# The sum of squares of a LayerNorm moved from ScalarE to VectorE, in an attention and feed-forward kernel

## Chip, cores and metric

The kernel runs on one Trainium2 chip, on all 8 of its cores. Each core does the same work on its own eighth of the data; the cores don't talk to each other. The metric is device time in microseconds (us) of the slowest core.

## The reference

The input x is 16 sequences of 4096 tokens, 1024 features each, in float32. One layer is computed:

```python
q, k, v = x @ Wq + bq, x @ Wk + bk, x @ Wv + bv      # 16 heads of 64
# local attention: a window of 128 tokens looks at itself and the window before it,
# causal, scale 64**-0.5; the first window of a sequence sees itself alone
a = softmax(mask(q k^T / 8)) v
x = layernorm(x + a @ Wo + bo)                        # no gain, no bias, eps 1e-5
x = layernorm(x + x @ W^T + b + (x @ V_r) @ C^T)      # V_r, C: rank 32
```

layernorm(y) is (y - mean) / sqrt(var + eps) over the 1024 features.

## The kernel before

**Work of a core.** A core has 2 sequences, 64 windows of 128 tokens; tokens lie on the 128 partitions. Weights are loaded once and cast to bf16 (the first 195 us or so, with the first x and its transposes). Then one loop runs over gi = 0 ... 65. Iteration gi does the attention of window gi, the output projection and first LayerNorm of window gi-1, and the feed-forward part and second LayerNorm of window gi-2. In every fourth iteration (gi = 0, 4, ..., 60) the projections q, k, v of four windows at once stand ahead of the attention (lines 640 to 685): 256 matmuls of 512 columns, in groups of 8 that take turns in four PSUM banks, p0, p1, ps2, ps3. This text calls them the projection block.

**Order.** Every instruction is emitted by hand in a fixed order for each engine, and each engine works through its own list in that order. `KB.emit` turns the tokens of producers and readers into waits on semaphores. VectorE, ScalarE and GpSimd also wait on their own last instruction before each new one (`CHAINED`). So an instruction on VectorE never starts before the one ahead of it in VectorE's list is done.

**One iteration**, in the order of the lists:

- TensorE: transposes of the attention output `ao` (line 377) and of the normed `x2b` (408); the projection block where due; scores (709), 8 groups; low-rank part (426); output projection (394), 16 matmuls, which this text calls the sweep; softmax sums (766); attention times v (808); low-rank second part (475) and feed-forward (488), 16 matmuls.
- ScalarE: copies of v after the projection block (678); 8 exponentials (730), each on one of 4 score banks; then the ScalarE part of the first LayerNorm (541, 556, 560, 569, 578) and of the second (541, 556, 560, 578).
- VectorE: copies out of the transposes (383, 414); bias adds of the projection block (656); copy of the low-rank part (432); causal mask (747); reciprocal of the sums (774); residual add of the first LayerNorm with row sums (454, two halves); first LayerNorm (537 to 563); scaling of the attention output into `ao` (825, two halves); residual add of the second (514, two halves); second LayerNorm (537 to 563).
- GpSimd: output DMA (526), prefilling y1 with x plus bias (441) and y2 (499), casts of x (595), copies of the last k and v (629, 634).

**LayerNorm** is `_ln`, called once for y1 and once for y2, so 128 times in all. VectorE adds the two half sums (537). ScalarE squares y (128 x 1024, float32) and sums the squares into a column `C_VAR` (541); the squared values themselves go to `aofm` as bf16 and nobody reads them. VectorE squares the sum (548) and forms the variance (551). ScalarE takes logarithm and exponential for the reciprocal root (556, 560). VectorE forms -mean times that (563). ScalarE writes the normed rows (569 for bf16, 578 for float32). The columns in between are all in one small tile `cols`.

The first residual add waits for the reciprocal in VectorE's list; the next iteration's exponentials stand behind line 578 of the second LayerNorm in ScalarE's list; the fourth and later score groups wait for a bank that an exponential has read.

Of the kernel before, what the change touches and what calls it, by code (L numbers as in the profile page):

```python
# [10 lines left out]
AF = mybir.ActivationFunctionType  # L11
ALU = mybir.AluOpType
# [91 lines left out]
def build_program(n_windows=64):  # L104
# [22 lines left out]
    kb = KB()  # L127
# [35 lines left out]
    aofm = S("aofm", [128, NCH, W], BF16)  # L163
# [30 lines left out]
    R = {name: Res() for name in  # L194
         ["xb0", "xb1", "xb2", "xb3", "xfm", "qfm", "kfm", "kprev", "v",
          "vprev", "ao", "aofm", "r16", "y1", "y2",
          "x2_0", "x2_1", "x2b_0", "x2b_1", "x2fm_0", "x2fm_1", "xr",
          "u0", "u1", "p0", "p1", "stgA", "stgB", "stgC",
          "cols1", "cols2", "ident", "m01", "ones"]}
# [8 lines left out]
    with ctx:  # L208
        t = kb.emit("gp", lambda e: e.memset(ident[:], 0.0), inc="gp")
        t = kb.emit("gp", lambda e: e.affine_select(  # L210
            out=ident[:], in_=ident[:], compare_op=ALU.not_equal, fill=1.0,
            base=0, pattern=[[-1, 128]], channel_multiplier=1),
            waits=[t], inc="gp")
# [3 lines left out]
            out=m01[:], in_=m01[:], compare_op=ALU.is_gt, fill=1.0,  # L217
            base=0, pattern=[[-1, 128]], channel_multiplier=1),
            waits=[t], inc="gp")
# [36 lines left out]
        for oc in range(NCH):  # L256
            buf, res = stg[i % 2]
            tok = kb.emit("sy", lambda e, s=wf_h[oc * 128:(oc + 1) * 128, :], b=buf:
                          e.dma_start(out=b[:], in_=s), waits=res.wr(),
                          inc=f"di{i % 2}", n=16)  # L260
            res.did_wr(tok)
            tok = kb.emit("ve", lambda e, b=buf: e.tensor_copy(out=xb[:, 0, :], in_=b[:]),
                          waits=res.rd() + R["xb0"].wr(), inc="ve")
# [7 lines left out]
                for ci in range(NCH)]  # L271
            tok = kb.group("pe", fns,
                           waits=R["xb0"].rd() + R["ident"].rd() + R["p0"].wr(),
                           inc="pe")
            R["xb0"].did_rd(tok)
            R["p0"].did_wr(tok)
            tok = kb.emit("ac", lambda e, oc=oc, pb=p0bf: e.activation(
                wt[:, :, oc * 128:(oc + 1) * 128],
                pb[0:128, 0:1024].rearrange("p (c f) -> p c f", c=NCH), AF.Copy),
                waits=R["p0"].rd(), inc="ac")  # L280
# [3 lines left out]
        for oc in range(NCH):  # L284
            buf, res = stg[i % 2]
            tok = kb.emit("sy", lambda e, s=cm_h[oc * 128:(oc + 1) * 128, :], b=buf:
                          e.dma_start(out=b[:, 0:32], in_=s), waits=res.wr(),
                          inc=f"di{i % 2}", n=16)
            res.did_wr(tok)
            tok = kb.emit("ve", lambda e, b=buf: e.tensor_copy(  # L290
                out=xb[:, 0, 0:32], in_=b[:, 0:32]),
                waits=res.rd() + R["xb0"].wr(), inc="ve")
# [3 lines left out]
            tok = kb.emit("pe", lambda e, pb=p1bf: e.transpose(  # L296
                pb[0:32, 0:128], xb[:, 0, 0:32], ident[:]),
                waits=R["xb0"].rd() + R["ident"].rd() + R["p1"].wr(), inc="pe")
            R["xb0"].did_rd(tok)
            R["p1"].did_wr(tok)  # L300
            tok = kb.emit("ac", lambda e, oc=oc, pb=p1bf: e.activation(
                ct[:, oc * 128:(oc + 1) * 128], pb[0:32, 0:128], AF.Copy),
                waits=R["p1"].rd(), inc="ac")
# [3 lines left out]
        for src_h, dst in [(bq_h, bqc), (bk_h, bkc), (bv_h, bvc)]:  # L307
            for c in range(NCH):
                tok = kb.emit("sy", lambda e, s=src_h[c * 128:(c + 1) * 128], d=dst, c_=c:
                              e.dma_start(out=d[:, c_:c_ + 1],  # L310
                                          in_=s.rearrange("(p o) -> p o", o=1)),
                              inc="dc", n=16)
                w_toks.append(tok)
        tok = kb.emit("sy", lambda e: e.dma_start(out=bo_row, in_=bo_h.rearrange("(o f) -> o f", o=1)), inc="dc", n=16)
        w_toks.append(tok)
        tok = kb.emit("sy", lambda e: e.dma_start(out=bf_row, in_=bf_h.rearrange("(o f) -> o f", o=1)), inc="dc", n=16)
# [3 lines left out]
                          waits=[("dc", rows_di)], inc="ve")  # L320
        for half in range(2):
# [7 lines left out]
                for ci in range(NCH)]  # L329
            tok = kb.group("pe", fns,  # L330
                           waits=[bvb_tok] + w_toks[24:32] + bres.wr(), inc="pe")
            bres.did_wr(tok)
            tok = kb.emit("ve", lambda e, b=bank, h=half: e.tensor_tensor(
                out=bo_row[0:1, h * 512:(h + 1) * 512], in0=b[0:1, 0:512],
                in1=bo_row[0:1, h * 512:(h + 1) * 512], op=ALU.add),
                waits=bres.rd() + [("dc", rows_di)], inc="ve")
            bres.did_rd(tok)
            kb.emit("ve", lambda e, h=half: e.tensor_copy(
                out=bcomb[:, h * 512:(h + 1) * 512],
                in_=bo_row[0:1, h * 512:(h + 1) * 512]), inc="ve")  # L340
        bffn_tok = kb.emit("ve", lambda e: e.tensor_copy(out=bffn[:], in_=bf_row),
                           waits=[("dc", rows_di)], inc="ve")
        for row_bf, bc in [(bcomb, bcomb_bc), (bffn, bffn_bc)]:
            for half in range(2):
                bank = p0 if half == 0 else p1
                bres = R["p0"] if half == 0 else R["p1"]
                tok = kb.emit("pe", lambda e, b=bank, h=half, rb=row_bf: e.matmul(
                    b[:], ones_r[:], rb[:, h * 512:(h + 1) * 512],
                    start=True, stop=True),
                    waits=[("ve", kb.cnt["ve"])] + bres.wr() + R["ones"].rd(),  # L350
                    inc="pe")
                bres.did_wr(tok)
                tok = kb.emit("ve", lambda e, b=bank, h=half, d=bc: e.tensor_copy(
                    out=d[:, h * 512:(h + 1) * 512], in_=b[:]),
                    waits=bres.rd(), inc="ve")
# [175 lines left out]
        def _ln(yres, ybuf, out_f32, out_bf, also_bf, out_res=None,  # L531
                bf_res=None, f32_res=None):
            if not isinstance(out_f32, bass.AP):
                out_f32 = out_f32[:]
            if out_bf is not None and not isinstance(out_bf, bass.AP):
                out_bf = out_bf[:]
            tok = kb.emit("ve", lambda e: e.tensor_tensor(
                out=cols[:, C_SUM:C_SUM + 1], in0=cols[:, C_SUM0:C_SUM0 + 1],
                in1=cols[:, C_SUM1:C_SUM1 + 1], op=ALU.add),
                waits=R["cols1"].rd(), inc="ve")  # L540
            tok = kb.emit("ac", lambda e: e.activation(  # L541
                aofm[:].rearrange("p c f -> p (c f)"), ybuf[:], AF.Square,
                accum_out=cols[:, C_VAR:C_VAR + 1]),
                waits=yres.rd() + R["aofm"].wr() + R["cols2"].wr(), inc="ac")
            yres.did_rd(tok)
            R["aofm"].did_wr(tok)
            sq_tok = tok
            kb.emit("ve", lambda e: e.tensor_tensor(
                out=cols[:, C_M2:C_M2 + 1], in0=cols[:, C_SUM:C_SUM + 1],
                in1=cols[:, C_SUM:C_SUM + 1], op=ALU.mult), inc="ve")  # L550
            tok = kb.emit("ve", lambda e: e.scalar_tensor_tensor(
                out=cols[:, C_VAR:C_VAR + 1], in0=cols[:, C_M2:C_M2 + 1],
                scalar=-1.0 / D, in1=cols[:, C_VAR:C_VAR + 1],
                op0=ALU.mult, op1=ALU.add),
                waits=[sq_tok], inc="ve")
            tok = kb.emit("ac", lambda e: e.activation(  # L556
                cols[:, C_LNV:C_LNV + 1], cols[:, C_VAR:C_VAR + 1], AF.Ln,
                bias=eps_c[:], scale=1.0 / D),
                waits=[tok] + R["ones"].rd(), inc="ac")
            rstd_tok = kb.emit("ac", lambda e: e.activation(  # L560
                cols[:, C_RSTD:C_RSTD + 1], cols[:, C_LNV:C_LNV + 1], AF.Exp,
                scale=-0.5), inc="ac")
            nmr_tok = kb.emit("ve", lambda e: e.tensor_scalar(
                out=cols[:, C_NMR:C_NMR + 1], in0=cols[:, C_SUM:C_SUM + 1],
                scalar1=cols[:, C_RSTD:C_RSTD + 1], scalar2=-1.0 / D,
                op0=ALU.mult, op1=ALU.mult), waits=[rstd_tok], inc="ve")
            R["cols2"].did_wr(nmr_tok)
            if also_bf:
                tok = kb.emit("ac", lambda e, o=out_bf: e.activation(
                    o, ybuf[:], AF.Identity, bias=cols[:, C_NMR:C_NMR + 1],  # L570
                    scale=cols[:, C_RSTD:C_RSTD + 1]),
                    waits=[nmr_tok] + yres.rd() + bf_res.wr(), inc="ac")
                yres.did_rd(tok)
                bf_res.did_wr(tok)
            w_extra = out_res.wr() if out_res is not None else []
            if f32_res is not None:
                w_extra = w_extra + f32_res.wr()
            tok = kb.emit("ac", lambda e, o=out_f32: e.activation(  # L578
                o, ybuf[:], AF.Identity, bias=cols[:, C_NMR:C_NMR + 1],
                scale=cols[:, C_RSTD:C_RSTD + 1]),  # L580
                waits=[nmr_tok] + yres.rd() + w_extra, inc="ac")
            yres.did_rd(tok)
            if out_res is not None:
                out_res.did_wr(tok)
            if f32_res is not None:
                f32_res.did_wr(tok)
            if also_bf:
                R["cols2"].did_rd(tok)
# [23 lines left out]
        for gi in (range(NW + 2) if PHASE >= 1 else []):  # L612
# [12 lines left out]
            if att and wt_ == 0:  # L625
# [16 lines left out]
                for dst, wmat, bias, dres in [(qfm, wq, bqc, R["qfm"]),  # L642
                                              (kfm, wk, bkc, R["kfm"])]:
                    for co in range(NCH):
# [4 lines left out]
                            for ci in range(NCH)]  # L649
# [9 lines left out]
                                          op0=ALU.add),  # L659
# [251 lines left out]
```

How the kernel before makes its waits and increments, by code:

```python
        def run(engine_obj, eng_name):  # L845
            for fn, ws, inc_sem, inc_n in kb.ops[eng_name]:
                for sname, val in ws:
                    engine_obj.wait_ge(sems[sname], val)
                inst = fn(engine_obj)
                if inc_sem:
                    inst.then_inc(sems[inc_sem], inc_n)
```

## Time and profile before

| | |
|---|---|
| median of 3 runs | 2299.39 us (2298.78 to 2299.47) |
| the profiled execution, its own time | 2299.96 us |
| its span, slowest core (core 1) | 2298.4 us (the eight: 2289.9 to 2298.4) |
| mean granted TensorE clock, every core | 0.869 to 0.870 |
| busy: TensorE matmul | 1729.3 us (75%) |
| busy: ScalarE | 855.5 us (37%) |
| busy: VectorE | 783.8 us (34%) |
| busy: GpSimd | 419.8 us (18%) |

Busy is the time in which an engine had an instruction running, as a share of the span. No engine is full. The granted clock is the share of 2.4 GHz that TensorE was given: in any moment it is 1 (2.4 GHz) or 0.5 (1.2 GHz). The span starts with the first instruction and ends with the last; the run's own time has 1.6 us around it.

### The profile page before, as it was taken

The page shows a single profiled execution, that of the slowest core. Times are in us where ns is not written, and L with a number is a line of the kernel's source. Part 1 is how long each engine was busy: PE and PEld are TensorE (multiplying, and loading weights), DVE is VectorE, ACT ScalarE, POOL GpSimd, SP SyncE. Part 2 cuts the span into 40 slices and gives each one's busy share as a digit, 9 for nine tenths or more (in the row PEclk, how much of TensorE's full clock was granted, in tenths as well). Part 3 has the DMA queues.
Part 4 walks back from the last instruction along what each step waited for, and adds up shares of the span by engine and source line. Part 5 has one row for each costly group of instructions (what it writes and reads, how often), then busy time and mean ns, then how long its engine had stood idle before and what let it go on. Part 6 is the DMA issues. An engine that isn't in the chain of part 4 may idle for free.

```text
span 2298.4 us, 37165 instructions; the slowest of 8 cores (2289.9 to 2298.4 us)
## 1 busy us (share of the span) xinstructions
PE 1729.3 (75%) x12924; PEld 884.8 (38%) x12924; DVE 783.8 (34%) x1774; ACT 855.5 (37%) x1381; POOL 419.8 (18%) x297
## 2 busy tenths in 40 slices
PE   0026787887969787787969787887969787887965
PEld 0012444444434444444434343444434444444432
DVE  1112243424333342424343343423333343424332
ACT  2110425335252434434252434435252434434253
POOL 0010022211131221212131221212131221212121
PEclk9987798888979798898989798888979898888977
DMA  5521010201111110201111110201111110201000
GB/s 184 161 70 48 19 56 23 70 12 37 46 47 47 32 62 16 70 18 38 47 47 47 33 61 17 76 11 37 46 47 46 32 61 17 77 10 38 10 29 28
DMA packets 111292, 107.58 MB, mean 47 GB/s; under 512 B 89602, under 2 KB 89602, under 8 KB 111108
## 3 DMA queue, kind: packets, MB, share of 16 engines
q1 hardware_dynamic: 101892, 71.66, 10.9%
q0 software_dynamic: 9216, 33.56, 3.7%
q8 instruction: 105, 1.72, 0.3%
q14 instruction: 79, 0.65, 0.1%
HBM read 54.81 MB, written 33.55 MB: 38 GB/s over the span
## 4 chain that ended last, share of the span: by engine, by line
PE 51%; ACT 20%; DVE 13%; issue 7%; DMA 5%; SPq 2%; DVEq 1%; ACTq 1%; POOL 0%; POOLq 0%
PE p L394 15%; PE p L646 10%; PE ps L646 10%; ACT ep L730 8%; ACT aofm L541 6%; PE ps L668 5%; PE p L668 5%; DVE ao L825 4%; DVE y L454 3%; DVE y L514 3%; PE ps L426 3%; ACT outb L578 3%; PE u L766 2%; SPq L602 2%; ACT cols L556 1%
## 5 line engine op out<-in xcount | busy, mean ns | idle before, releaser
L709 PE MATMUL ps<-qfm,kfm 64*128 64x128 bf16 x1792 | 180.5, 254 | 250.7 <-ACT ep L730 247.3
L394 PE MATMUL p<-wo,aofm 128*128 128x512 bf16 x1024 | 343.0, 510 | 0.0
L541 ACT ACTIVATE aofm<-y 128x1024 bf16<-128x1024 f32 x128 | 135.3, 1057 | 522.7 <-DVE y L454 347.8
L730 ACT ACTIVATE ep<-ps 128x512 bf16<-128x512 f32 x496 | 296.2, 597 | 83.5 <-PE ps L709 8.4
L526 POOL DMA_DIRECT2D out<-outb x64 | 36.7, 573 | 1584.6 <-DVE x2fm L414 1460.4
L488 PE MATMUL p<-wt,x2fm 128*128 128x512 bf16 x1024 | 233.9, 382 | 0.0
L678 ACT CAST v_sb<-p 128x512 bf16<-128x512 f32 x64 | 37.5, 586 | 523.7 <-PE p L668 523.7
L709 PEld LDWEIGHTS ps<-qfm,kfm 64*128 64x128 bf16 x1792 | 110.2, 107 | 299.5 <-issue 294.7
L394 PEld LDWEIGHTS p<-wo,aofm 128*128 128x128 bf16 x1024 | 122.4, 125 | 201.7 <-issue 159.8
L432 DVE CAST xr<-ps 32x128 bf16<-32x128 f32 x64 | 17.8, 279 | 498.9 <-PE ps L426 498.9
L441 POOL TENSOR_TENSOR y<-x_sb,bcomb_bc 128x1024 f32<-128x1024 f32 x64 | 136.5, 2133 | 63.9 <-ACT x L578 59.8
L646 PE MATMUL p<-xfm,wq 128*128 128x512 bf16 x512 | 118.3, 385 | 36.4 <-DMA xfm<-xb 36.4
L488 PEld LDWEIGHTS p<-wt,x2fm 128*128 128x128 bf16 x1024 | 95.3, 98 | 123.1 <-issue 18.4
L499 POOL TENSOR_TENSOR y<-x,bffn_bc 128x1024 f32<-128x1024 f32 x64 | 135.8, 2122 | 12.9 <-POOL y L441 12.7
L668 PE MATMUL ps<-wv,xfm 128*128 128x512 bf16 x512 | 115.7, 379 | 0.0
L646 PE MATMUL ps<-xfm,wq 128*128 128x512 bf16 x512 | 115.7, 379 | 0.0
L646 PE MATMUL p<-xfm,wk 128*128 128x512 bf16 x512 | 115.7, 379 | 0.0
L646 PE MATMUL ps<-xfm,wk 128*128 128x512 bf16 x512 | 115.7, 379 | 0.0
L668 PE MATMUL p<-wv,xfm 128*128 128x512 bf16 x512 | 115.7, 379 | 0.0
L595 POOL CAST xb<-x_sb 128x1024 bf16<-128x1024 f32 x64 | 78.1, 1220 | 201.1 <-DMA x_sb<-x 191.2
L747 DVE TENSOR_TENSOR ep<-ep,m 128x2048 bf16<-128x2048 bf16 x64 | 87.8, 1373 | 74.7 <-ACT ep L730 56.5
L514 DVE SCALAR_TENSOR_TENSOR y<-p,y 128x512 f32<-128x512 f32 x128 | 88.5, 691 | 31.5 <-DVE ao L825 13.9
(89 smaller groups left out, 2012.8 us busy)
## 6 DMA issues: line engine op xcount, KB each, us to landing
x_sb<-x SPq DMA_DIRECT2D x16, 2048.0 KB, 8.3
out<-outb POOLq DMA_DIRECT2D x64, 512.0 KB, 3.1
xfm<-xb SPq DMA_TRANSPOSE x512, 2.3
y<-Wq SPq DMA_DIRECT2D x8, 512.0 KB, 4.3
y<-Wk SPq DMA_DIRECT2D x8, 512.0 KB, 4.0
y<-Wv SPq DMA_DIRECT2D x8, 512.0 KB, 4.5
y<-Wo SPq DMA_DIRECT2D x8, 512.0 KB, 4.6
y<-Wf SPq DMA_DIRECT2D x8, 512.0 KB, 4.3
```

The costliest lines, as they stand in the source:

```text
L394: fns = [(lambda e, ci=ci, b=bank, h=half: e.matmul(b[:], aofm[:, ci, :], wo[:, ci, h * 512:(h + 1) * 512], start=(ci == 0), stop=(ci == N ...
L441: tok = kb.emit("gp", lambda e, w_=wt_, p_=par: e.tensor_tensor(out=y1[:], in0=x_sb[:, p_, w_, :], in1=bcomb_bc[:], op=ALU.add), waits=R[" ...
L488: fns = [(lambda e, ci=ci, b=bank, h=half, pw=pw: e.matmul(b[:], x2fm[:, pw, ci, :], wt[:, ci, h * 512:(h + 1) * 512], start=False, stop=( ...
L499: tok = kb.emit("gp", lambda e, pw=pw: e.tensor_tensor(out=y2[:], in0=x2[:, pw, :], in1=bffn_bc[:], op=ALU.add), waits=R["y2"].wr() + R[f" ...
L514: e.scalar_tensor_tensor(out=y2[:, h * 512:(h + 1) * 512], in0=b[:], scalar=1.0, in1=y2[:, h * 512:(h + 1) * 512], op0=ALU.mult, op1=ALU.a ...
L541: tok = kb.emit("ac", lambda e: e.activation(aofm[:].rearrange("p c f -> p (c f)"), ybuf[:], AF.Square, accum_out=cols[:, C_VAR:C_VAR + 1] ...
L646: fns = [(lambda e, ci=ci, b=bank, co=co, wm=wmat: e.matmul(b[:], wm[:, ci, co * 128:(co + 1) * 128], xfm[:, ci, :], start=(ci == 0), stop ...
L668: fns = [(lambda e, ci=ci, b=bank, tc=tc, h=half: e.matmul(b[:], xfm[:, ci, tc * W:(tc + 1) * W], wv[:, ci, h * 512:(h + 1) * 512], start= ...
L709: e.matmul(b[:, r:r + 128], ks, qs, start=True, stop=True))
L730: tok = kb.emit("ac", lambda e, b=bank, g=g: e.activation(ep[:, g, :], b[:], AF.Exp, scale=0.125), waits=bres.rd() + eres.wr(), inc="ac")
L747: tok = kb.emit("ve", lambda e, epc=ep_cur: e.tensor_tensor(out=epc, in0=epc, in1=m01[:].unsqueeze(1).broadcast_to([128, 16, 128]), op=ALU ...
L825: tok = kb.emit("ve", lambda e, b=bank, bi=bank_i: e.tensor_tensor(out=ao[:, bi * 512:(bi + 1) * 512].rearrange("p (h f) -> p h f", h=8), ...
```

## The change

In `_ln` the squares and their sum are made by VectorE, in one `scalar_tensor_tensor` instruction that computes (y * 1.0) * y and sums it, in place of ScalarE's `activation` with `AF.Square`. Output tile, accumulated column, waits and readers are the same; the token is VectorE's. In VectorE's list the instruction stands behind line 537 and ahead of line 548.

```diff
@@ _ln
                 in1=cols[:, C_SUM1:C_SUM1 + 1], op=ALU.add),
                 waits=R["cols1"].rd(), inc="ve")
-            tok = kb.emit("ac", lambda e: e.activation(
-                aofm[:].rearrange("p c f -> p (c f)"), ybuf[:], AF.Square,
+            tok = kb.emit("ve", lambda e: e.scalar_tensor_tensor(
+                out=aofm[:].rearrange("p c f -> p (c f)"), in0=ybuf[:],
+                scalar=1.0, in1=ybuf[:], op0=ALU.mult, op1=ALU.mult,
                 accum_out=cols[:, C_VAR:C_VAR + 1]),
-                waits=yres.rd() + R["aofm"].wr() + R["cols2"].wr(), inc="ac")
+                waits=yres.rd() + R["aofm"].wr() + R["cols2"].wr(), inc="ve")
             yres.did_rd(tok)
             R["aofm"].did_wr(tok)
             sq_tok = tok
```

## Rows read from the trace of the kernel before

**Rows 1.** The page's chain that ended last: by engine, then by line.

```profile
PE 51%; ACT 20%; DVE 13%; issue 7%; DMA 5%; SPq 2%; DVEq 1%; ACTq 1%; POOL 0%; POOLq 0%
PE p L394 15%; PE p L646 10%; PE ps L646 10%; ACT ep L730 8%; ACT aofm L541 6%; PE ps L668 5%; PE p L668 5%; DVE ao L825 4%; DVE y L454 3%; DVE y L514 3%; PE ps L426 3%; ACT outb L578 3%; PE u L766 2%; SPq L602 2%; ACT cols L556 1%
```

**Rows 2.** Groups of instructions: count | busy us, mean ns | idle before, releaser.

```profile
L394 PE MATMUL p<-wo,aofm 128*128 128x512 bf16 x1024 | 343.0, 510 | 0.0
L541 ACT ACTIVATE aofm<-y 128x1024 bf16<-128x1024 f32 x128 | 135.3, 1057 | 522.7 <-DVE y L454 347.8 <-PE p L475 100.6 <-DVE y L514 66.2
L454 DVE SCALAR_TENSOR_TENSOR y<-p,y 128x512 f32<-128x512 f32 x128 | 88.5, 691 | 21.4 <-DVE r L774 8.3 <-PE p L394 4.9
L747 DVE TENSOR_TENSOR ep<-ep,m 128x2048 bf16<-128x2048 bf16 x64 | 87.8, 1373 | 74.7 <-ACT ep L730 56.5 <-ACT ep L724 18.2
...
L240 DVE CAST wk<-y 128x1024 bf16<-128x1024 f32 x4 | 2.8, 694 | 18.9 <-DMA y<-Wk 18.9
```

**Rows 3.** VectorE's timeline, iteration 26; last, projection block of gi 28: start, us.

```profile
1062.29 0.69 DVE L454 SCALAR_TENSOR_TENSOR y<-p,y 128x512 f32<-128x512 f32 x1
...
1063.09 0.16 DVE L537 TENSOR_TENSOR cols<-cols 128x1 f32<-128x1 f32 x1
1063.36 0.16 DVE L548 TENSOR_TENSOR cols<-cols 128x1 f32<-128x1 f32 x1
1064.39 0.16 DVE L551 SCALAR_TENSOR_TENSOR cols<-cols 128x1 f32<-128x1 f32 x1 [0.87 <-ACT aofm L541]
...
1068.39 0.69 DVE L514 SCALAR_TENSOR_TENSOR y<-p,y 128x512 f32<-128x512 f32 x1 [0.17 <-DVE y L514]
...
1069.20 0.16 DVE L537 TENSOR_TENSOR cols<-cols 128x1 f32<-128x1 f32 x1
...
1070.44 0.16 DVE L551 SCALAR_TENSOR_TENSOR cols<-cols 128x1 f32<-128x1 f32 x1 [0.82 <-ACT aofm L541]
...
1096.47 0.75 DVE L656 TENSOR_SCALAR qfm<-p,bqc 128x512 bf16<-128x512 f32 x1 [0.18 <-DVE x2fm L414]
```

**Rows 4.** Timeline of ScalarE in iteration 26 and into 27.

```profile
1063.14 1.06 ACT L541 ACTIVATE aofm<-y 128x1024 bf16<-128x1024 f32 x1 [6.27 <-DVE y L454]
1064.10 0.19 ACT L541 ACTIVATION_READ_ACCUMULATOR aofm<-y 128x1 f32 x1
...
1069.19 1.06 ACT L541 ACTIVATE aofm<-y 128x1024 bf16<-128x1024 f32 x1 [0.91 <-DVE y L514]
...
1073.14 5.81 ACT L730 ACTIVATE ep<-ps 128x512 bf16<-128x512 f32 x8
```

**Rows 5.** The chain: start, us; sweeps of iterations 4, 21-23, 57-60; projection block gi 28.

```profile
359.52 4.36 PE p L394 x16
...
902.59 5.87 PE p L394 x16
926.50 5.86 PE p L394 x16
950.06 4.34 PE p L394 x16
...
1098.40 3.45 PE p L646 x16
...
2066.21 4.35 PE p L394 x16
2088.24 5.26 PE p L394 x16
2111.55 5.55 PE p L394 x16
2172.45 5.82 PE p L394 x16
```

**Rows 6.** Two of those sweeps as stretches: busy us of each engine, PEclk, DMA.

```profile
926.50:932.36 5.86, 5.86 (x24) 2.24 (x24) 1.50 (x2) 0.94 (x2) 0.73 (x1) 0.60 0.11 24
950.06:954.40 4.34, 4.34 (x24) 1.85 (x24) 1.51 (x2) 0.93 (x2) 0.73 (x1) 0.82 0.01 4
```

## The prediction

> **What bounds the kernel now.** I read the shares of the engines first: none is full. The chain of work that ended last therefore came next. It has TensorE at 51%, ScalarE at 20%, VectorE at 13% and 7% of issue, spread over a dozen lines; the ScalarE square (line 541) alone holds 6% of the span [rows 1]. A chain that keeps changing engines means latency: each step waits for the one before it. The question is whether the square is on that chain in all iterations, and what the replacement takes.
>
> The groups say what the square waits for. ScalarE sat idle 522.7 us ahead of its 128 squares, and the releasers are VectorE's residual adds (454, 514) [rows 2]; the 14 put down to line 475 are the same wait, since 475 itself waits for line 454. ScalarE never holds its square back in the loop. In the timeline of iteration 26 ScalarE had been idle 6.27 us before the first square and 0.91 us before the second [rows 4]. VectorE in turn stood idle 0.87 and 0.82 us for it, with line 551 starting 0.10 us after the sum was read out (1064.10 + 0.19, then 1064.39) [rows 3, 4]. So ScalarE has room, and relieving it of 135 us buys nothing by itself. What counts is when line 551 can start.
>
> From line 551 on all is serial. First LayerNorm: 551, 556, 560, 563, then 825 (which stands behind 563 in VectorE's list), then 514. Second: 551 to 563, then ScalarE's 578, then the exponentials that stand behind it (1073.14 in iteration 26 [rows 4]), of which the fifth frees the bank for line 426, behind which the sweep stands. The sweep ends in line 766, the reciprocal and the next 454. A delay of either line 551 goes into the iteration whole.
>
> One place has cover. In the 15 iterations that a projection block follows, the next user of the second LayerNorm is line 656. The first one starts at 1096.47 and takes 0.75, so bank p0 is free at 1097.22; TensorE wants it at 1098.40 [rows 3, 5]. That is 1.18 us of slack, and the exponentials come a whole block later. So 64 first LayerNorms and 64 - 15 = 49 second ones are exposed.
>
> **The cost, step by step.** Removed: 1.06 us on ScalarE, and 0.19 for reading the sum, overlapping to 1.15 (1063.14 to 1064.29) [rows 4].
>
> Added: one VectorE instruction, 128 x 1024, two float32 sources in SBUF, with a sum. No row has this form. The nearest is line 454, the same operation with a sum over 512 columns, one source in PSUM: 0.691 us [rows 2]. One column costs 0.16 us (line 551) [rows 3], so a column costs (0.691 - 0.159) / 511 = 1.04 ns and 1024 take 0.159 + 1023 x 0.00104 = 1.22 us. Bounds: below, the one-source copy of 1024 float32 columns, 0.694 (line 240); above, two of line 454, 1.38. The two-source bf16 line 747 has 2048 columns in 1.373 us [rows 2], half the cost of a column; it isn't float32. I take 1.22, the same operation and type. The readout of the sum lies inside that, as in 454.
>
> Queue position: the square can't start beside line 537 as before (1063.14), but behind it.
>
> - First LayerNorm: 537 at 1063.09, so the square takes the place of 548, 1063.36, and ends 1064.58. The gap behind a sum is 0.11 (454 ends 1062.98, 537 starts 1063.09), so 548 starts 1064.69 and, 0.27 later, 551 at 1064.96. Before: 1064.39. Delay 0.57 us: 0.22 of later start, 0.07 of longer work, and the rest is 548, which was hidden behind the square and now stands in line, with the wait for ScalarE (0.10) saved.
> - Second LayerNorm: 537 at 1069.20, square at 1069.47, end 1070.69, 548 at 1070.80, 551 at 1071.07, against 1070.44 [rows 3]: 0.63 us.
>
> Plain sum: 64 x 0.57 + 49 x 0.63 = 36.5 + 30.9 = 67 us. With the bounds for the square the delays are 0.04 and 0.10 (plain sum 7 us) or 0.73 and 0.79 (85 us).
>
> Costed at nothing: ScalarE's end of it (the second square now waits, over `cols`, for line 578 of the first; that ends 0.91 us ahead of 1069.19 [rows 4], at 1068.28, and the square can't start before 1069.47, so 1.2 us of cover); tile `aofm` as a dump, since its reader, the sweep, is over before 454 starts and its next writer, 383, is VectorE's own; GpSimd, which works in neither LayerNorm.
>
> **What TensorE's clock gives back.** The sweep is 16 matmuls and takes 4.34 us at a mean granted clock of 0.82 and 5.86 at 0.60 [rows 5, 6]: it starts at 1.2 GHz, after a stretch in which TensorE was mostly idle, and ends at 2.4. How much of it is slow depends on where its start falls. Rows 5 show a rule. Two sweeps that start 23.91 us apart are alike (5.87, 5.86). From 2066.21 to 2088.24 is 22.03 and the sweep grows by 0.91; from there to 2111.55 is 23.31 and it grows by 0.29. So the next sweep is longer by half of what the distance lacks to 23.9. Over a projection block: 60.90 from 2111.55 to 2172.45, growth 0.27, so 60.90 + 0.54 = 61.44 repeats. The rule stays within sweeps of some 4.3 to 6.0 us; a sweep that would pass the upper end comes back at the lower, as 5.86 is followed by 4.34. Before, the iteration is too short to settle: fixed part 22.03 - 4.35 = 17.68, which would need a sweep of 6.2.
>
> After, the fixed part is 17.68 + 1.20 = 18.88 and a sweep of 5.02 makes 23.9; with the block, 60.90 - 5.55 = 55.35, plus 0.57, and 5.52 makes 61.44. Both lie inside, so the distances settle at 3 x 23.9 + 61.44 = 133.1 us for four windows. Before, 14 such groups took 2172.45 - 359.52 = 1812.9, or 129.5 each [rows 5]. That is 3.6 x 14 = 51 us. Before iteration 4 stand three first LayerNorms and one exposed second: 3 x 0.57 + 0.63 = 2.3, of which I take 2. Behind the sweep of iteration 60 stand five first and six second: 2.9 + 3.8 = 6.6, less about 1 for shorter sweeps. Sum 51 + 2 + 5.5 = 58.5; as the sweeps need not start where they end, I take 57. Of the plain 67, about 10 come back through shorter sweeps: their mean falls from (129.5 - 3 x 17.68 - 55.35) / 4 = 5.28 to (133.1 - 3 x 18.88 - 55.92) / 4 = 5.14.
>
> The profiled execution took 2299.96 us and the median is 2299.39, 0.6 less. 2299.96 + 57 = 2357.0; I give 2357 us.
>
> **Rivals.**
>
> *Half rate.* The square takes two cycles a column: 0.159 + 1023 x 0.00208 = 2.29 us, delays 1.64 and 1.70, and the block's slack of 1.18 is passed by 0.52 in 15 iterations. Plain: 105 + 83 + 8 = 196. The 64 sweeps of 5.28 now may go to either end, 4.35 or 6.0: -60 to +46 us; a middle of 5.2 gives -5. Time about 2491, from 2436 to 2542. For it: no row here has two float32 sources in SBUF over more than one column. Against it: all 512-column float32 rows run at one rate. The Trainium skill (Vector Engine (DVE) Microarchitecture Reference, section 7, Points that are easy to get wrong) says just this: the scalar-tensor-tensor form with two non-bf16 SBUF sources halves throughput. By that page the square would last about 2.3 us, and the time would be this rival's; no run here shows it yet. Another page (VectorE: DVE Perf Modes, the section on the errata) has a float32 two-source add at 2048 columns in 2.291 us, one column a cycle, and by it the 1.22 above would hold. 12 in 100.
>
> *No change.* The square runs two columns a cycle, as line 240's copy seems to: 0.69 us, delays 0.04 and 0.10, 7 us plain, and the sweeps hardly move: about 2304, give or take 6. It decides from 0.65 us downwards: then line 551 is released earlier than by ScalarE and the kernel gets faster by 1 us for every 0.01. For it: ScalarE's handover goes. Against: two sources, and line 454 shows the operation at one column per 1.04 ns. 6 in 100 (a third of it faster than 0.2%).
>
> *The clock takes, not gives.* The gaps of TensorE grow from both sides of the transposes, and the sweeps go to 6.0 instead of settling: 67 + 64 x 0.7 = +112, 2412 us. Against: rows 5's rule. 5 in 100.
>
> **Chances and range.** Forecast 77 (2335 to 2375: the square between 1.0 and 1.4, with all or none of the clock's return), half rate 12, no change 6, clock 5. 2335 to 2385 holds the forecast and a share of the mixed outcomes toward the clock's rival, about 80. A measurement of this kernel tells 0.2%, 4.6 us, from no change. Faster 2, within 3, slower 95.
>
> **What would show it.** Line 541 on VectorE, 128 times, near 1.22 us, 0.27 behind 537; from 537 to 551 1.87 us (1.30 and 1.24 now); ScalarE's idle time before 556, not 541. Sweeps near 5.0 in plain iterations and 5.5 behind a block, starts 23.9 apart; line 656 still free of waits into the block. ScalarE busy down by about 147 us (128 x 1.15), VectorE up by 156. The prediction is wrong if the square is near 0.7 or 2.3 us, if second LayerNorms turn out covered (31 us less), or if starts don't settle at 23.9.

## The result

The changed kernel takes 2355.96 us (median of 8 runs) against 2300.1 us for the kernel before (10 runs): 55.9 us more. The ratio is 1.0228, with a 95% interval of 1.0204 to 1.0252. The forecast was 2357 us. In some runs, of either kernel, the cores of one die had a lower granted clock than the others (2475.21 us, 0.79 to 0.80 against 0.87); ratios and intervals in this text leave these slow runs out and medians don't, which moves a median by 2 us at most, but for one where both are given (without them the two here are 2354.21 and 2299.64, 54.6 apart). The profiled execution took 2354.21 us, its span is 2352.7 us on core 0.

The page of the changed kernel, shares of the engines and then the chain by engine and by line:

```profile
PE 1711.2 (73%) x12924; PEld 876.4 (37%) x12924; DVE 941.7 (40%) x2030; ACT 708.1 (30%) x1125; POOL 419.9 (18%) x297
...
PE 58%; DVE 14%; ACT 12%; issue 6%; DMA 5%; SPq 2%; POOL 1%; DVEq 1%; ACTq 1%; POOLq 0%
PE p L394 13%; PE p L647 10%; PE ps L647 9%; PE p L488 9%; ACT ep L731 8%; PE ps L669 5%; PE p L669 5%; DVE y L454 3%; DVE aofm L541 3%; DVE y L514 3%; ACT outb L579 2%; PE ps L426 2%; DVE ao L826 2%; PE u L767 2%; SPq L603 2%
```

VectorE has 157.9 us more work and ScalarE 147.4 less, nearly one for one, and the kernel is slower all the same: busy shares said nothing of it. The chain of [rows 1] had ScalarE's square at 6%; here VectorE's has 3% and line 488 has 9%, where it wasn't among the lines listed before. That last entry misleads. In the timeline below the second half of line 826 (at 1086.85) stands 0.17 us behind the first, as VectorE's instructions do that wait for nothing but what is long done (the first half, behind line 564), and line 488 happens to end just then; the chain is traced back through TensorE there instead of through the LayerNorm. All lines behind 541 have moved by one: 551 is 552, 646 is 647.

The groups of the changed kernel:

```profile
L557 ACT ACTIVATE cols<-cols,eps_c 128x1 f32<-128x1 f32 x128 | 37.7, 294 | 782.8 <-DVE cols L552 782.8
L541 DVE SCALAR_TENSOR_TENSOR aofm<-y 128x1024 bf16<-128x1024 f32 x128 | 156.9, 1225 | 19.9 <-DVE cols L537 12.7
```

The square takes 1225 ns where 1.22 us was forecast. ScalarE's idle time has moved from line 541 (522.7 us, [rows 2]) to line 557 (782.8).

VectorE's timeline in iteration 26, which answers to [rows 3]:

```profile
1081.99 0.69 DVE L454 SCALAR_TENSOR_TENSOR y<-p,y 128x512 f32<-128x512 f32 x1
...
1082.79 0.16 DVE L537 TENSOR_TENSOR cols<-cols 128x1 f32<-128x1 f32 x1
1083.06 1.23 DVE L541 SCALAR_TENSOR_TENSOR aofm<-y 128x1024 bf16<-128x1024 f32 x1
1084.21 0.08 DVE L541 DVE_READ_ACCUMULATOR aofm<-y 128x1 f32 x1
1084.39 0.16 DVE L549 TENSOR_TENSOR cols<-cols 128x1 f32<-128x1 f32 x1
1084.66 0.16 DVE L552 SCALAR_TENSOR_TENSOR cols<-cols 128x1 f32<-128x1 f32 x1
...
1085.99 0.69 DVE L826 TENSOR_TENSOR ao<-u,r 128x512 bf16<-128x512 f32 x1 [0.17 <-DVE cols L564]
1086.85 0.69 DVE L826 TENSOR_TENSOR ao<-u,r 128x512 bf16<-128x512 f32 x1 [0.17 <-PE p L488]
...
1089.46 0.16 DVE L537 TENSOR_TENSOR cols<-cols 128x1 f32<-128x1 f32 x1
1089.80 1.23 DVE L541 SCALAR_TENSOR_TENSOR aofm<-y 128x1024 bf16<-128x1024 f32 x1 [0.17 <-DVE cols L537]
...
1091.40 0.16 DVE L552 SCALAR_TENSOR_TENSOR cols<-cols 128x1 f32<-128x1 f32 x1
```

From 537 to the variance is 1.87 us in the first LayerNorm (1.30 before), and 1.94 in the second (1.24 before). So the delays are 0.57, as forecast, and 0.70 instead of 0.63: the second square starts 0.34 behind 537, not 0.27, because it has one more wait to carry out (ScalarE's line 579, over `cols`). In this trace each wait ahead of a VectorE instruction adds some 0.07 us even where what it waits for is long done: the idle time is 0.11 us ahead of the first square, with one wait, and 0.17 ahead of the second, with two.

The sweeps in the changed kernel's chain (iterations 20 to 22, 24 to 28), which answer to [rows 5]:

```profile
893.14 5.25 PE p L394 x16
917.21 5.30 PE p L394 x16
941.46 5.12 PE p L394 x16
...
1026.25 5.25 PE p L394 x16
1050.31 5.30 PE p L394 x16
1074.92 4.95 PE p L394 x16
1098.82 4.95 PE p L394 x16
1159.48 5.25 PE p L394 x16
```

Plain iterations are now 24.07 (893.14 to 917.21), 24.25, 24.61 and 23.90 us apart, where they were 22.03 to 23.91 before. Four windows take 1026.25 - 893.14 = 133.1 and 1159.48 - 1026.25 = 133.2 us; forecast was 133.1.

### The profile page after: what moved, and what is told of

Its sections match the earlier page's. It is cut to its first block, busy times and chain, and to the rows that moved or that the text cites. A ratio compares the mean times of both kernels' runs of the same rounds, so it can differ in the third digit from the quotient of the medians.

```text
span 2352.7 us, 36908 instructions; the slowest of 8 cores (2347.4 to 2352.7 us)
## 1 busy us (share of the span) xinstructions
PE 1711.2 (73%) x12924; PEld 876.4 (37%) x12924; DVE 941.7 (40%) x2030; ACT 708.1 (30%) x1125; POOL 419.9 (18%) x297
## 4 chain that ended last, share of the span: by engine, by line
PE 58%; DVE 14%; ACT 12%; issue 6%; DMA 5%; SPq 2%; POOL 1%; DVEq 1%; ACTq 1%; POOLq 0%
PE p L394 13%; PE p L647 10%; PE ps L647 9%; PE p L488 9%; ACT ep L731 8%; PE ps L669 5%; PE p L669 5%; DVE y L454 3%; DVE aofm L541 3%; DVE y L514 3%; ACT outb L579 2%; PE ps L426 2%; DVE ao L826 2%; PE u L767 2%; SPq L603 2%
## 5 line engine op out<-in xcount | busy, mean ns | idle before, releaser
L394 PE MATMUL p<-wo,aofm 128*128 128x512 bf16 x1024 | 331.0, 496 | 0.0
L557 ACT ACTIVATE cols<-cols,eps_c 128x1 f32<-128x1 f32 x128 | 37.7, 294 | 782.8 <-DVE cols L552 782.8
L541 DVE SCALAR_TENSOR_TENSOR aofm<-y 128x1024 bf16<-128x1024 f32 x128 | 156.9, 1225 | 19.9 <-DVE cols L537 12.7
```

The costliest lines, as they stand in the source:

```text
L394: fns = [(lambda e, ci=ci, b=bank, h=half: e.matmul(b[:], aofm[:, ci, :], wo[:, ci, h * 512:(h + 1) * 512], start=(ci == 0), stop=(ci == N ...
L541: tok = kb.emit("ve", lambda e: e.scalar_tensor_tensor(out=aofm[:].rearrange("p c f -> p (c f)"), in0=ybuf[:], scalar=1.0, in1=ybuf[:], op ...
```

## The experiments

The *plain sum* is what the delays add up to if each counts in full: 67 us, or 71 with the 0.70 found above. Two theories stood against each other for the fact that about 55 us were measured. *Settling*: the sweeps give back whatever keeps four windows at 133.1 us. *Fixed share*: 0.83 of each delay is seen (56 of 67). Times are medians; "above" and "below" are against the kernel before in the same session (2300.6, 2301.1 and 2300.7 us in the three).

### One LayerNorm at a time

In the cuts of code from here on, `...` stands for what is left out.

```diff
-            tok = kb.emit("ac", ... AF.Square ...)
+            if also_bf:        # first LayerNorm; "not also_bf" in the second run
+                tok = kb.emit("ve", ... scalar_tensor_tensor ...)
+            else:
+                tok = kb.emit("ac", ... AF.Square ...)
```

> VectorE makes the squares in the first LayerNorm only; the second keeps ScalarE's. Line 551 is late by 0.57 us in 64 first LayerNorms. Theory (the starts of the sweeps settle): the fixed part of a plain iteration is 17.68 + 0.57 = 18.25, a sweep of about 5.6 fills it up to 23.9, so four windows take the same 133.1 us as with both squares moved, and the run is 48 to 55 us above before. Rival (a fixed share of every delay is given back, 56 us for a plain sum of 67, or 0.83): 0.83 x 36.5 = 30 us above before.

Measured: 2333.01 us, 32 above, ratio 1.015 (1.012 to 1.018).

> VectorE makes the squares in the second LayerNorm only. Line 551 is late by 0.63 us in 49 exposed second LayerNorms. Theory (settling): fixed part 17.68 + 0.63 = 18.31, sweep about 5.6, distance 23.9; the iteration with the projection block behind it gets no delay of its own. 40 to 54 us above before. Rival (fixed share): 0.83 x 30.9 = 26 us. A third: if second LayerNorms are not exposed at all, under 5 us.

Measured: 2352.04 us, 51 above, ratio 1.0228 (1.0213 to 1.0243).

The two don't agree on a theory: the first says fixed share, the second says settling. The second LayerNorm alone costs nearly as much as both. The chain of the run with the first LayerNorm alone (core 1) shows why; these are the sweeps behind projection blocks, four windows apart, from the early and the later part:

```profile
355.24 5.52 PE p L394 x16
...
488.25 5.58 PE p L394 x16
...
621.37 5.58 PE p L394 x16
...
1416.42 3.56 PE p L394 x16
...
1546.13 3.56 PE p L394 x16
```

488.25 - 355.24 = 133.0 and 621.37 - 488.25 = 133.1; but 1546.13 - 1416.42 = 129.7. Away from the start of the second sequence (gi 32) four windows take a time near one of two values in this run. Where the sweep behind the block takes 3.56 us, at a granted clock of 1.00, it is about 129.7; where it takes longer (5.58 us at 0.64) it is about 133.1. The delays are the same throughout. The short sweep goes along with the lower value but doesn't make it: the kernel before takes 129.7 too (129.5 on the mean, [rows 5]) with sweeps of 4.4 to 5.9 us behind its blocks. So the sweeps do settle, but at one of two distances, and a small delay gets the lower one part of the time. The eight cores of this run spread from 2309.9 to 2326.4 us: three of them have the lower value in the first four groups of four windows and five the upper, and from there on all do alike. In the run with the second alone the sweeps behind blocks on core 1 start at 354.07 and 487.17, 133.1 apart, and it keeps to that (132.9 on the mean of 14 groups). Why a delay in the second LayerNorm holds the upper value throughout and one in the first doesn't isn't shown by these runs.

### A little more and a little less

Both runs start from the changed kernel. The first adds an instruction of one column on VectorE, the second moves one from VectorE to ScalarE.

```diff
             kb.emit("ve", ... C_M2 ...)
+            kb.emit("ve", lambda e: e.tensor_tensor(
+                out=cols[:, 12:13], in0=cols[:, C_SUM:C_SUM + 1],
+                in1=cols[:, C_SUM:C_SUM + 1], op=ALU.mult), inc="ve")
```

> The changed kernel with one more VectorE instruction on one column (about 0.27 us start to start) behind line 549 in each LayerNorm: nothing is computed with it. Plain cost 0.27 x 113 = 30 us. Theory (settling): the fixed part goes from 18.9 to 19.4, the sweep shrinks from 5.1 to about 4.6 and the starts stay 24 apart: 0 to 4 us above the changed kernel. Rival (fixed share): 25 us above it.

Measured: 2373.74 us, the median of 2372.03, 2373.74 and 2394.96 (2384.35 with a fourth of 2542.63, whose clock fell to 0.76 to 0.77 on half of the cores), ratio 1.0366 (1.0312 to 1.042). That is 73 above the kernel before and 20 above the changed one. In the two lower runs all eight cores have a granted clock of 0.89, in the third only four, so 18 to 20 is the better size. No run is within the 0 to 4 of settling, and the fixed share's 25 is missed too. The chain of the slowest core (core 7) shows what happened; these are the sweeps of iterations 22 to 24:

```profile
943.48 4.50 PE p L394 x16
967.82 5.97 PE p L394 x16
1030.04 5.58 PE p L394 x16
```

The sweeps shrink to some 4.5 us, as settling says, and then one takes 5.97. Six of the 14 groups of four windows take 132.6 to 133.6 us, near the value of the changed kernel; the other eight have such a long sweep or come right behind it, and take 134.0 to 134.9. So settling holds in this trace only until the sweeps have shrunk to about 4.5 us.

```diff
-            kb.emit("ve", ... C_M2 = C_SUM * C_SUM ...)
+            m2_tok = kb.emit("ac", lambda e: e.activation(
+                cols[:, C_M2:C_M2 + 1], cols[:, C_SUM:C_SUM + 1], AF.Square),
+                waits=[sum_tok], inc="ac")
```

> The changed kernel with the square of the sum (line 549, one column) made by ScalarE beside VectorE's long square, so it no longer stands in VectorE's line. It takes 0.27 us off each LayerNorm's path. Theory (settling): fixed part 18.9 - 0.54 = 18.3, the sweep grows by as much: 0 to 3 us below the changed kernel. Rival (fixed share): 25 us below it.

Measured: 2325.34 us, 25 above the kernel before (ratio 1.0108, 1.0091 to 1.0125) and 31 below the changed one. This too is against settling as first stated. It takes 0.2 us off each delay in the timeline, not 0.27, as the step behind the square now has a wait more; plain that is 23 us. The rest comes from groups of four windows that fall back from 133.1 to 129.7: on core 1 eight of 14 take 128.9 to 130.3 us, and six 132.5 to 133.9. Its sweeps behind blocks are of both kinds, as in the run with the first LayerNorm alone.

### Taking the clock out of it

If the clock is what gives back and takes away, keeping TensorE at work in its long gap should leave the plain delays. The gap is between the fourth score group and the fifth, the first that waits for a bank which an exponential has read (the text on the kernel before says the fourth); it is some 4.8 us in the kernel before.

```diff
             for g in range(8):
                 bank, bres = ps[g % 4], R[f"s{g % 4}"]
+                if gi >= 2 and g >= 4:
+                    nd = 16 if (g == 4 and wt_ != 0) else 1
+                    fns = [(lambda e: e.matmul(
+                        p0[:], ident[:], wq[:, 0, 0:512],
+                        start=True, stop=True)) for _ in range(nd)]
+                    R["p0"].did_wr(kb.group("pe", fns, waits=R["p0"].wr(), inc="pe"))
```

The results of these matmuls are overwritten unread. The kernel before and the changed one get the same edit.

> The kernel before, with extra matmuls of 512 columns into bank p0 while TensorE has nothing to do: 16 ahead of the fifth score group (1 where the projection block has just run), 1 ahead of each of the next three. Nobody reads their results. If the clock is what makes the sweep long, it now runs at 2.4 GHz throughout, 3.63 us as the shortest sweeps of the other runs, in place of 5.36 on the mean: 64 x 1.7 = 109 us below before, about 2190. Rival: the extra matmuls run at 1.2 GHz themselves (16 x 0.43 = 6.9 us in a gap of 4.8) and delay the scores: 48 x 2 = 96 us lost, about what is gained, 2290.

Measured: 2212.36 us, 89 below, ratio 0.9611 (0.9595 to 0.9628). The theory of the clock holds, the forecast of 109 was too high: part of the sweeps stayed long (on core 1, 22 of 64, and the mean fell from 5.36 to 4.02 us).

> The same extra matmuls in the changed kernel. With the clock held up nothing can be given back by sweeps, so the distance to the kernel before with the extra matmuls is the plain sum of the delays: 64 x 0.57 + 49 x 0.63 = 67 us. If less is exposed than counted (a theory that the 56 us measured are the true exposure and the clock has no part), the distance is 56 again.

Measured: 2305.7 us, 93 above the kernel before with the same extra matmuls (against the kernel before the ratio is 1.0022, 1.0012 to 1.0032). Neither 67 nor 56. In the timeline of TensorE on core 1 the gap is not filled:

```profile
1066.92 3.63 PE L696 MATMUL p<-wq,ident 128*128 128x512 bf16 x16
1072.52 0.38 PE L716 MATMUL ps<-qfm,kfm 64*128 64x128 bf16 x4 [1.97 <-ACT ep L737]
...
1076.44 4.75 PE L394 MATMUL p<-wo,aofm 128*128 128x512 bf16 x16
```

After 16 extra matmuls TensorE still waits 1.97 us, and the sweep takes 4.75. The changed kernel has a longer gap, so the same extra work protects it less: its sweeps on core 1 take 4.40 us on the mean against 4.02, and the plain 71 with 64 x 0.38 = 24 us of longer sweeps is 95, near the 93. The comparison had to be made with filled gaps: 21 extra matmuls before, 24 with the squares of the second LayerNorm (or both) on VectorE.

> The kernel before with 21 extra matmuls in the gap in place of 16, so that less than 0.5 us of it stays empty. With 16 some 23 of 64 sweeps were still longer than 3.63 us. Theory (the clock sets the sweep, the delays count in full): nearly all sweeps at 3.63, so 10 to 25 us below the version with 16, about 2190 to 2200. Rival (the extra matmuls themselves get in the way): 5 x 0.21 us x 48 = 50 us above it.

Measured: 2182.25 us, ratio 0.949 (0.9473 to 0.9506), 118 below the kernel before. Lower than expected.

> The changed kernel with 24 extra matmuls in its gap, which is 0.63 us longer. With 16, 2 us of the gap stayed empty and most sweeps took 4.3 to 4.9. Theory: sweeps at 3.63 here too, and the distance to the kernel before with a filled gap is the plain sum, 67 us (60 to 74), about 2262. Rival (exposure is not what was counted): 93 us as between the two versions with 16, or 56 as between the two kernels.

Measured: 2265.45 us, ratio 0.9855 (0.9835 to 0.9874), 83 above the filled kernel before by the medians, outside the 60 to 74 that were expected. The profiled executions are nearer. The views of cores, filled before and then filled after:

```profile
die 0 (median of its cores): 2178.1 us, clock 0.971
die 1 (median of its cores): 2176.2 us, clock 0.972
```

```profile
die 0 (median of its cores): 2251.7 us, clock 0.959
die 1 (median of its cores): 2253.1 us, clock 0.960
```

On the median core that is 73.6 and 76.9 us. Sweeps in the two chains on core 1, again filled before and then filled after:

```profile
353.59 3.56 PE p L394 x16
...
1449.57 3.56 PE p L394 x16
1470.29 3.56 PE p L394 x16
...
2060.82 3.56 PE p L394 x16
```

```profile
355.66 3.56 PE p L394 x16
...
400.79 4.77 PE p L394 x16
...
1621.31 3.56 PE p L394 x16
1643.29 3.56 PE p L394 x16
...
2126.83 3.56 PE p L394 x16
```

The first and last row of each are iterations 4 and 60, 14 groups of four windows apart, so four windows take 121.94 and 126.51 us: 4.57 more. The plain sum is 4 x 0.57 + 3 x 0.70 = 4.38. The middle rows are one iteration of each, the first behind a block, at a granted clock of 1.00: 20.72 and 21.98 us, 1.26 more, which is 0.57 + 0.70. With the clock nearly out of it, the delays count in full; what is left over are long sweeps such as the 4.77 (clock 0.959 against 0.971), and they make the medians of the slowest core differ by more than the cores in general.

> Squares on VectorE in the second LayerNorm alone, gap filled with 24. Theory: 49 x 0.63 = 31 us above the kernel before with a filled gap (27 to 37), though without the filling the same change cost 52. Rival (the second LayerNorm's delay costs more than its own size for a reason that is not the clock): 52 again.

Measured: 2237.22 us, ratio 0.9732 (0.9694 to 0.9771), 55 above the filled kernel before, where 49 x 0.70 = 34 is the corrected plain sum. On the median core of the profiled executions it is 47 and 50. Its clock is lower too (0.961 to 0.966 against 0.970 to 0.972), and that is where the rest goes. From core 1: the sweeps of iterations 56 and 57 in the chain, then iteration 21 as a stretch (the third number from the end is the granted clock), and the feed-forward matmuls in it:

```profile
1974.53 3.56 PE p L394 x16
1995.94 3.56 PE p L394 x16
```

```profile
873.59:895.87 22.28, 21.15 (x184) 10.78 (x182) 10.64 (x25) 10.65 (x18) 9.79 (x8) 0.92 0.17 46
```

```profile
880.74 5.31 PE L488 MATMUL p<-wt,x2fm 128*128 128x512 bf16 x16
```

From sweep to sweep iteration 56 takes 21.41 us, at a granted clock of 1.00. That is 0.69 above the 20.72 of the filled kernel before: the delay, and no more. The extra time is in iterations in which the clock fell, by a sweep of 4.8 to 5.1 us or by a feed-forward (line 488) of up to 5.31 in place of 3.63. Between iterations 4 and 60 core 1 has 19 such iterations with this change and 10 in the filled kernel before. So the rival, a reason that isn't the clock, isn't borne out; why the clock falls more often with this change isn't shown.

### A version that is faster than both

Another way to a shorter path is to let ScalarE keep the square and start it earlier, in halves, and let VectorE fold the first half with the mean's square meanwhile. `half0` is the token of the first half of line 454 or 514. The two lines with `#` stand for the code of two VectorE instructions.

```diff
+            for half, col in ((0, 10), (1, C_VAR)):
+                tok = kb.emit("ac", lambda e, h=half, c=col: e.activation(
+                    aofm[:, 4 * h:4 * h + 4].rearrange("p c f -> p (c f)"),
+                    ybuf[:, h * 512:(h + 1) * 512], AF.Square,
+                    accum_out=cols[:, c:c + 1]),
+                    waits=([yres.half0] if half == 0 else yres.rd())
+                    + R["aofm"].wr() + R["cols2"].wr(), inc="ac")
+                sqs.append(tok)
...
+            # VectorE: cols 11 = C_M2 * (-1 / D) + cols 10, waits=[sqs[0]]
+            # VectorE: C_VAR = cols 11 + C_VAR, waits=[sqs[1]]
```

> The kernel before, squares on ScalarE, but in two halves of 512 columns: the first as soon as VectorE has the first half of the residual add, and VectorE folds it with the mean's square while ScalarE does the second half. On the path stands a half square of about 0.65 to 0.75 us instead of 1.15: 0.43 x 113 = 49 us below before. Where the four-window distance moves only in steps (129.7 and 133.1 us were seen), 7 x 0.43 = 3.0 us of shorter fixed part in four windows is nearly one step of 3.4: 0 if it stays, 48 to 55 if it steps.

Measured: 2250.28 us, 51 below, ratio 0.9779 (0.9762 to 0.9796). ScalarE has more to do in it (161.2 us of squares against 135.3), and the kernel is faster. The group, two rows of ScalarE's timeline and two of VectorE's (here 541 is the line that was 537, and 564 forms the variance):

```profile
L547 ACT ACTIVATE aofm<-y 128x512 bf16<-128x512 f32 x256 | 161.2, 630 | 429.0 <-DVE y L454 291.2
```

```profile
1043.22 0.63 ACT L547 ACTIVATE aofm<-y 128x512 bf16<-128x512 f32 x1 [6.66 <-DVE y L454]
...
1044.15 0.63 ACT L547 ACTIVATE aofm<-y 128x512 bf16<-128x512 f32 x1 [0.20 <-DVE cols L541]
```

```profile
1043.98 0.16 DVE L541 TENSOR_TENSOR cols<-cols 128x1 f32<-128x1 f32 x1
...
1044.97 0.16 DVE L564 TENSOR_TENSOR cols<-cols 128x1 f32<-128x1 f32 x1 [0.23 <-ACT aofm L547]
```

From the sum to the variance is 0.99 us here, against 1.30 before, and 0.93 against 1.24 in the second LayerNorm: 0.31 us shorter in both, not 0.43, for VectorE's four small instructions in a row take nearly as long as the second half of the square. Plain that is 113 x 0.31 = 35 us. The expectation's 49 came out by luck: some 15 of the 51 us are the clock's.

> Halved squares and extra matmuls together. If both act on different parts of the chain they add: 109 + 49 = 158 us below before, about 2142.

Measured: 2163.43 us, 138 below, ratio 0.9407 (0.9389 to 0.9426), where 158 was expected. 89 and 51 add to 140, but 51 holds a part that the clock gives in the kernel without extra matmuls, so the sum doesn't show that the two act on different things.

> Halved squares on ScalarE, gap filled with 19. Theory: 0.45 x 113 = 50 us below the kernel before with a filled gap, about 2145; the version with 16 was at 2163 with some long sweeps left.

Measured: 2151.72 us, ratio 0.9361 (0.9345 to 0.9378). It is the fastest here, 149 below the kernel before and 204 below the changed one. Against the filled kernel before it gains 31 (31.4 on the median core of the profiled executions), not 50. That is near the plain 35 of the 0.31 us above: the sweeps are at their floor in both, and the clock has little more to add.

## Why the prediction was right

*ScalarE's relief buys nothing.* Right. It lost 147.4 us of work, and what moved is its idle time, from line 541 to 557.

*The price of the square.* Right: 1225 ns measured, 1.22 us forecast from the slope between line 551 and line 454. The rival of half rate fell with it. The Trainium skill (Vector Engine (DVE) Microarchitecture Reference, section 7) has two non-bf16 SBUF sources at half throughput; this trace doesn't agree, with 1225 ns for 1024 float32 columns, both sources the same tile. The Trainium skill's other page (VectorE: DVE Perf Modes, the errata section) gives a formula for a float32 two-source add, one column a cycle; by it 1024 columns take 1224 ns, an estimate, and this trace agrees, with 1225.

*Delays.* 0.57 in the first LayerNorm was exact. The term for the second was mis-sized: 0.63 forecast, 0.70 measured, as the extra wait was seen (it was costed at nothing for what it waits for) but not its own 0.07 us. The plain sum is then 64 x 0.57 + 49 x 0.70 = 71, not 67.

*Exposure.* 64 and 49 hold by the filled pair, 4.57 us in four windows against 4.38, and 1.26 in one iteration against 1.27. That second LayerNorms ahead of a projection block are covered holds too, barely. From the changed kernel's VectorE timeline and then its chain, block of gi 24:

```profile
985.51 0.75 DVE L657 TENSOR_SCALAR qfm<-p,bqc 128x512 bf16<-128x512 f32 x1 [0.18 <-DVE x2fm L414]
```

```profile
986.41 3.61 PE p L647 x16
```

Bank p0 is free at 986.26 and wanted at 986.41; this stretch is one of three among 15 blocks where the fifth group was late by 0.17 us (3.61 against 3.45, [rows 5]). In the others the slack went from 1.0 us or so to 0.3. The prediction had 1.18 for it, as it took the start from the chain; TensorE's own timeline has the fifth group 0.16 us earlier, and the slack of gi 28 is 1.02.

*What the clock gives back.* That it gives back a part was right, and the size nearly (about 10 us forecast; with the corrected sum 71 - 54.3, the profiled spans' difference, is 17), and so was the distance of four windows, 133.1. The steps to it were partly wrong. Plain iterations came out mostly at 24.1 to 24.6 rather than 23.9, which the prediction itself had named as a sign of being wrong, and sweeps behind a block at 5.25 rather than 5.5; that the two errors cancel in the four-window distance is luck. And the rule isn't that any delay in range settles at 133.1: the experiments show two values that come again, 129.7 and 133.1, mixtures of both, and others (134.0 to 134.9 with the extra instruction, 126.3 on the mean with halved squares). The forecast for both squares fell on the upper one of the two. Of those made by the same rule for other sizes, the one for the second square alone held (40 to 54, measured 51), and those for the first alone, for the padding and for line 549 on ScalarE missed. The prediction's total is right by its main terms, but its account of the clock was only good for this one size.

*Ends.* 12 of the 14 groups between iterations 4 and 60 sit at 133.1 on the mean; the two around gi 32, where a new sequence starts, were shorter, so these 14 gave 47.5 us, not 51 ((2220.96 - 360.53) - (2172.45 - 359.52)). The start gave 1.0 (2 forecast), which says little, as the cores of the kernel before reach iteration 4 some 7 us apart; the tail gave 5.8 (5.5). That the total came within 1 us of 2357 is in part luck too: the prediction's own sum was 58.5, rounded to 57 without a term for it, and the profiled spans are 54.3 apart.

What stays open: why four windows come to 129.7 or 133.1 us, why the second LayerNorm's delay alone keeps to the upper value, and why the clock falls more often with it in the filled kernel. The first LayerNorm's change wasn't run with a filled gap.

## What to carry to other kernels

An engine with idle time is no reason to hand it work in a chain of dependent steps: ask what must now stand in line that stood beside. Here VectorE's square was only 0.07 us longer than ScalarE's, and the delay was 0.57, because line 537 and line 549 used to run beside it. In such a chain it can pay to split the long step so that its first half starts while its input is still being made: that was worth 51 us (2.2%) here, with more instructions, and 31 with the gap filled. And where a matmul engine idles for some 5 us in a loop, fill the gap before judging small changes: it was worth 118 us by itself, and it takes away most of what made a change of 35 us look like 51 here, and one of 71 like 55.

## What was not expected of the hardware

The time of four windows moved between two values, about 129.7 and 133.1 us, within one execution and with the work unchanged; in that run the lower one came with a sweep behind the block at a granted clock of 1.00, the upper with 0.64 or so. Equal cores of one execution ended up to 16 us apart, most of it for this (2309.9 to 2326.4). A wait whose condition was met long ago still cost VectorE 0.07 us. And extra matmuls that compute nothing, 21 in a gap of 4.8 us, made the kernel 5.1% faster (2182.25 against 2300.7 us), as the 16 matmuls behind them then ran in 3.56 us instead of 5.3.
